# Row maxima of two heads in 64-row pairs, with the odd heads' keys turned round in SBUF

## The reference

```
q, k = rotary(x @ wq.T), rotary(x @ wk.T)          # 4 x 16 heads x 1024 x 64
scores = q @ k.T / 8                               # causal: key <= query
probs  = softmax(where(causal, scores, -inf))      # subtracts each row's maximum
out    = probs @ v
```

## Time and profile before

| | us |
|---|---|
| median of 3 runs | 1261.14 (1259.26 to 1264.67) |
| the profiled execution, its own time | 1261.32 |
| its span | 1259.3 |
| PE busy | 1144.7 (91%) |
| DVE busy | 983.3 (78%) |
| ACT busy | 956.5 (76%) |
| POOL busy | 947.3 (75%) |

### The profile page before, as it was taken

The page is one execution under the profiler, slowest core; times in us unless marked ns, Lnnn a source line. Parts: engine busy times, 40 slices in busy tenths (PEclk is TensorE's granted clock), DMA queues, the critical chain, the costliest instruction groups (busy, mean ns, idle before and its releaser), DMA issues. The chain is left out here.

```text
span 1259.3 us, 34888 instructions
## 1 busy us (share of the span) xinstructions
PE 1144.7 (91%) x13543; PEld 788.8 (63%) x13543; DVE 983.3 (78%) x2220; ACT 956.5 (76%) x2193; POOL 947.3 (75%) x984
## 2 busy tenths in 40 slices
PE   4689999999999999999999999999999598999996
PEld 1256676676767676767667676767777454566553
DVE  7798777787868797878778787979674559867987
ACT  3667888878787878787887879787979665766574
POOL 3578889889888989898988889898767475334463
PEclk8699999999999999999999999999999899999998
DMA  6652425243351515152515334251602100000011
GB/s 201 147 135 52 123 65 129 60 118 82 89 127 43 133 38 136 37 134 69 129 49 128 83 87 118 53 135 35 153 2 65 51 2 1 1 1 1 2 35 34
DMA packets 50660, 97.03 MB, mean 77 GB/s; under 512 B 6720, under 2 KB 23360, under 8 KB 48448
## 3 DMA queue, kind: packets, MB, share of 16 engines
q1 hardware_dynamic: 50496, 94.81, 30.2%
HBM read 58.47 MB, written 34.60 MB: 74 GB/s over the span
## 5 line engine op out<-in xcount | busy, mean ns | idle before, releaser
L807 POOL TENSOR_TENSOR Plo<-P,Phi 128x512 f16<-128x512 f32 (+3 forms) x640 | 538.3, 866 | 129.2 <-ACT P L498 128.6
L495 ACT ACTIVATE Phi<-psS 128x512 f16<-128x512 f32 (+3 forms) x768 | 384.0, 500 | 149.5 <-PE psS L353 105.9
L498 ACT ACTIVATE P<-psS 128x512 f32<-128x512 f32 (+3 forms) x640 | 307.0, 480 | 0.0
L347 PE MATMUL psS<-Q,K 128*128 128x512 f16 (+3 forms) x768 | 252.0, 328 | 40.5 <-DVE Plo L654 37.1
L374 PE MATMUL psO<-V,Plo 128*128 128x65 f16 x2304 | 288.7, 194 | 0.0
L370 PE MATMUL psO<-V,Phi 128*128 128x65 f16 x2304 | 287.5, 192 | 0.0
L372 PE MATMUL psO<-V,Phi 128*128 128x64 f16 x2304 | 286.6, 192 | 0.0
L703 DVE TENSOR_REDUCE pmax<-psX 128x1 f32<-128x512 f32 x384 | 252.9, 684 | 23.0 <-PE psX L434 14.3
L370 PEld LDWEIGHTS psO<-V,Phi 128*128 128x128 f16 x2304 | 219.5, 98 | 56.6 <-issue 0.4
L350 PE MATMUL psS<-Q,K 65*128 65x512 f16 (+3 forms) x768 | 252.2, 328 | 0.0
L434 PE MATMUL psX<-K,Q 128*128 128x512 f16 (+4 forms) x768 | 227.5, 332 | 11.7 <-DMA Q<-HL 3.8
(11 more groups left out here) (200 smaller groups left out, 2161.1 us busy)
## 6 DMA issues: line engine op xcount, KB each, us to landing
K<-k_way SPq DMA_DIRECT2D x48, 512.0 KB, 7.0
k_way<-HL SPq DMA_DIRECT2D x64, 256.0 KB, 3.7
q_way<-HL SPq DMA_DIRECT2D x60, 256.0 KB, 3.7
Q<-q_way SPq DMA_DIRECT2D x60, 256.0 KB, 7.1
Q<-q_way SPq DMA_DIRECT2D x15, 512.0 KB, 11.9
out<-y SPq DMA_DIRECT2D x8, 256.0 KB, 2.2
y<-in_x SPq DMA_DIRECT2D x3, 512.0 KB, 10.8
hn<-in_x SPq DMA_DIRECT2D x3, 512.0 KB, 5.5
```

What stands on the lines that cost most here:

```text
L347: nc.tensor.matmul(out, M.K1[:, p, h, j * P:(j + 1) * P], M.Q1[:, p, h, c:c + w], start=True, stop=False)
L495: nc.scalar.activation(M.Phi[:, U % NP_, 0:w], X, ACT.Exp, scale=SCALE)
L498: nc.scalar.activation(full, X, ACT.Exp, scale=SCALE).then_inc(S.exp_done, 1)
L807: nc.gpsimd.tensor_tensor(M.Plo[:, U % NP_, 0:w], M.P32[:, U % NP_, 0:w], M.Phi[:, U % NP_, 0:w], ALU.subtract).then_inc(S.lo_pool, 1)
```

## The change

The odd heads' keys are loaded turned round, low rows on partitions 0 to 63 and high rows on 64 to 127. This takes three transfers of keys for two heads where one stood, and the same bytes. The full 128-row products of the scores are the same sum in another order. The four banks of `MAXB` that hold a single product of 512 columns without a diagonal (`PAIRED`, banks 4 to 7) are made with the high rows alone: for an even head from partitions 0 to 63, for the odd head beside it from 64 to 127, the one directly behind the other (`both_heads`). The low half of the keys is left out of these products. The even head's item waits for both banks, then both products are issued. The first group's maxima (s < 0) are as before. In `plan()` the items of two heads alternate, and both items of a pair stand at the step of the first.

```diff
--- before.py
+++ after.py
@@ -70,6 +70,7 @@
 NMIX = 3
 assert sorted((t, j + i) for bank in MAXB for t, j, n in bank for i in range(n)) == [
     (t, j) for t in range(TT) for j in range(t + 1)]
+PAIRED = [k for k, bank in enumerate(MAXB) if [j + n - 1 < t for t, j, n in bank] == [True]]
 LO_LAG = 0
 LAG = 5
 NP_ = 6
@@ -128,15 +129,17 @@
                     at.setdefault(V_FIRST[tp], []).append((s, "v", tp))
                 else:
                     put(s, V_STEPS[tp], ("v", tp))
-            for h in range(GH):
-                for k in range(len(MAXB)):
-                    if s < 0:
-                        slot, u = MX_FIRST_GROUP[h]
+            if s < 0:
+                for h in range(GH):
+                    slot, u = MX_FIRST_GROUP[h]
+                    for k in range(len(MAXB)):
                         at.setdefault((slot, u + k), []).append((s, "mx", h, k))
-                    else:
-                        first, last = MX_SECOND if s == 0 else (MX_FIRST, MX_LAST)
-                        i = h * len(MAXB) + k
-                        put(s, first + i * (last - first) // (GH * len(MAXB) - 1), ("mx", h, k))
+            else:
+                first, last = MX_SECOND if s == 0 else (MX_FIRST, MX_LAST)
+                for i in range(GH * len(MAXB)):
+                    pair, k, odd = i // 2 // len(MAXB), i // 2 % len(MAXB), i % 2
+                    own = i - odd if k in PAIRED else i
+                    put(s, first + own * (last - first) // (GH * len(MAXB) - 1), ("mx", 2 * pair + odd, k))
             if s < 0:
                 for h in range(GH):
                     at.setdefault(MT_FIRST[h], []).append((s, "mt", h))
@@ -374,6 +377,23 @@
                     mm = nc.tensor.matmul(O, M.Plo[:, U % NP_, k * P:(k + 1) * P], V[:, HD:2 * HD + 1],
                                           start=False, stop=j == t, skip_group_check=True)
                 mm.then_inc(S.weighted_done, 1)
+
+            def both_heads(item):
+
+                s, kind, h, k = item
+                p = (s + 1) % 2
+                other = (s, kind, h + 1, k)
+                if number[other] >= NAUX:
+                    pe.wait_ge(S.aux_free[bank(other)], number[other] // NAUX)
+                c = 0
+                for t, j, n in MAXB[k]:
+                    for x, low in ((item, 0), (other, HD)):
+                        mm = nc.tensor.matmul(M.psX[:, bank(x), c:c + n * P],
+                                              M.Q1[low:low + HD, p, x[2], t * P:(t + 1) * P],
+                                              M.K1[low:low + HD, p, x[2], j * P:(j + n) * P], start=True, stop=True)
+                        if (t, j, n) == MAXB[k][-1]:
+                            mm.then_inc(S.aux_ready, 1)
+                    c += n * P
 
             def side(item):
                 s, kind, *a = item
@@ -426,7 +446,11 @@
                             pe.wait_ge(S.first_k, 32)
                             pe.wait_ge(S.first_q[h // 2], 16 * GH)
                         else:
-                            pe.wait_ge(S.near_in[h // 2], 48 * (s + 1))
+                            pe.wait_ge(S.near_in[h // 2], 80 * (s + 1))
+                    if s >= 0 and k in PAIRED:
+                        if h % 2 == 0:
+                            both_heads(item)
+                        return
                     c = 0
                     rows = HD if s < 0 and h == 0 else P
                     for t, j, n in MAXB[k]:
@@ -902,7 +926,9 @@
                 sp.wait_ge(S.q_out, 16 * GH * (s + 1))
                 for i in range(2):
                     h = slice(2 * i, 2 * i + 2)
-                    sp.dma_start(M.K1[:, p, h], krows[:, h]).then_inc(S.near_in[i], 16)
+                    sp.dma_start(M.K1[:, p, 2 * i], krows[:, 2 * i]).then_inc(S.near_in[i], 16)
+                    sp.dma_start(M.K1[0:HD, p, 2 * i + 1], krows[HD:P, 2 * i + 1]).then_inc(S.near_in[i], 16)
+                    sp.dma_start(M.K1[HD:P, p, 2 * i + 1], krows[0:HD, 2 * i + 1]).then_inc(S.near_in[i], 16)
                     sp.dma_start(M.Q1[0:HD, p, h], qrows[0:HD, h]).then_inc(S.near_in[i], 16)
                     sp.dma_start(M.Q1[HD:P, p, h], qrows[0:HD, h]).then_inc(S.near_in[i], 16)
                 sp.dma_start(M.K2[0:HD, p], krows[0:HD]).then_inc(S.far_in, 16)
@@ -918,7 +944,7 @@
                     sp.wait_ge(S.first_k2, 16)
                 if which == 0 and s >= 0:
                     for i in range(2):
-                        sp.wait_ge(S.near_in[i], 48 * (s + 1))
+                        sp.wait_ge(S.near_in[i], 80 * (s + 1))
                     sp.wait_ge(S.far_in, 32 * (s + 1))
                 for h in range(GH):
                     sp.dma_start(way[:, :, h, :].rearrange("k f n -> f k n"),
```

## The result

The changed kernel takes 1293.71 us (median of 4, 1292.58 to 1295.92), the one before 1260.2 (median of 4): the ratio is 1.0266, with a 95% interval of 1.0248 to 1.0284. That is 33.5 us slower. Forecast were 1278 and a range of 1252 to 1296; the direction was right, and the loss was forecast at half its size.

A forecast was written before the change was run, and what follows sets the result against it. PE alone was taken to bound steps 8 to 39, sharing the rest with ACT and POOL. Waits of 13 x 1.63 us plus 0.6 made 21.8; a quarter back left 16.4, so 1261.3 became 1278, range 1252 to 1296.

The forecast's parts named there:

- I take a quarter back: Over the groups, a quarter of the 21.8 us loss returns in PE's existing waits, leaving 16.4 us.
- A pair costs 0.43 us: At each pair on PE: 0.43 us against 0.44 for two full products, range 0.22 to 0.54.
- a count of clocks: At each switch to or from 64 rows: 0.05 to 0.057 us at 2.4 GHz, against 0.11 if a time.
- Step 18: At the pair, PE waits 0.84 us a group for DVE to free the first projection's bank.
- Step 19: At the wo item, PE waits 0.1 us at most for the second projection's bank; not counted.
- Step 21: At the wo item, PE waits 0.59 us a group for the bank of step 20's values' product.
- Step 32: Bank 5's pair waits for the first reduce of step 31: 0.2 us a group, 0 to 0.54.
- Steps 15 and 16: No PE wait forecast here; only DVE's low halves delayed 0.6 us at step 16, costing nothing or up to 0.3 a group.
- Loads: Two more load issues ahead of a group's first queries: nothing, at most 0.8 us a group where landing is late.
- one behind the other: Rival: a pair's products don't overlap and cost 0.13 to 0.23 us more than today; 1291, up to 1295 us; chance 0.12.
- absorbed and paying: Rival: PE's waits behind step 39 absorb the 1.63 us and each pair saves 0.10; 1249 us; chance 0.17.
- half and half: Rival: half of the new waits are absorbed (0.8) and each pair saves 0.05; 1266 us; chance 0.15.

The follow-up runs named there:

- e8: The changed kernel with the second wo product at step 22 instead of 21: 1285.34 us, ratio 1.0203 to the kernel before.
- e2: The kernel before with only the odd heads' turned keys, loaded in three transfers for one: 1259.95 us, ratio 0.9997.
- e4: The changed order with both products of a pair on rows 0 to 63, keys not turned, loads of before: 1303.57 us, ratio 1.034 to the kernel before.
- e7: The changed kernel with the first of step 18's two projections at step 17: 1294.84 us, ratio 1.0278 to the kernel before.
- e11: The changed kernel with the pairs of bank 5 one step later (16 to 17, 32 to 33): 1299.92 us, ratio 1.0324 to the kernel before.
- e1: The changed order and common wait, but both products of a pair over all 128 rows, keys and loads of before: 1293.87 us, ratio 1.0262 to the kernel before.
- e3: The kernel before with the 16 products a group that the change pairs each made alone over 64 rows: 1295.32 us, ratio 1.0268.
- e5: The changed kernel with its pairs at every second step (15 to 21 and 31 to 37): 1263.28 us, ratio 1.0031 to the kernel before.
- e6: Pairs at every second step as in e5, but full 128-row products, keys and loads of before: 1266.33 us, ratio 1.0061 to the kernel before.

## Why the prediction was right, and what was off

- *PE is the bound in steps 8 to 39, so a wait there costs its length*: right. "I take a quarter back" was about right in size, 0.4 us a group: the waits for score banks fell from 30.4 to 23.9 us, 0.5 a group. But it came back at step 31 (0.34 here), and nothing behind step 34 (2.42 there, 2.45 at step 47), where the prediction saw most of these waits.
- *A pair costs 0.43 us, which is no gain*: right. The two switches are 0.10 each and the second weight adds nothing; the reading "a time" held, and "a count of clocks", behind the rival that was to be 1249 us, didn't. The range of 0.22 to 0.54 held the value. Missed was that a wait can hide the switch into the pair, as at step 15: a pair there costs 0.32.
- *Step 18*: forecast 0.84 us. The step grew by 1.11 (0.36 to 1.47), of which 0.16 is the pair in the place of one masked product (0.43 against 0.27): 0.95.
- *Step 19*: a wait of 0.1 at most for the second projection's bank, "not counted". It is about 0.15 (by the table, 0.16: the difference fell by 0.06 where a product of 0.22 had left the step).
- *Step 21*: forecast 0.59. The loss grew by 0.67 from step 20 to 22, though a product of 0.22 has left step 21 and a pair has taken the place of one at step 20 (0.21 more): 0.68 or so. e8 took away 8.4 us, 0.65 a group.
- *Step 32*: forecast a net 0.20, in a range to 0.54. At equal work (steps 22 and 34) the loss went from 2.08 to 2.42. With the 0.34 that came back at step 31 that is some 0.7 lost at step 32: the reduce of step 30 that DVE still had before it was not counted.
- *Steps 15 and 16*: missed, 0.36 us by step 18. The prediction named 0.6 us more for DVE at step 16, but not the pair's second bank, that of the first reduce of step 15: some 0.3. The rest is the wait at step 15, 0.22 us for the reduce of step 14, less the 0.1 of the switch that it hides.
- *Loads*: right, nothing (e2).
- *The signs*: as forecast. PE waits 0.9 us for the first projection and 0.5 for the values once a group, the two products of a pair start together, the matmul behind them 0.32 later. The distance between two groups' loads grew from 57.9 to 60.5 us (439.52 to 499.98); forecast was 59.2.

The mechanism was right and the terms of the sum too small: 0.36 + 0.95 + 0.16 + 0.68 + 0.7 = 2.85 us in this group instead of 1.63. Less what came back that is 2.85 - 0.34 = 2.5, instead of 1.63 - 0.41 = 1.22. Over the 13 groups the mean is 2.27 against 1.22, 14 us more, and the group s = 14 cost 2.2 instead of 0.45. That makes 15.4 of the 17 us.

That 1294 lies within the range at all is luck. For this mechanism by itself the prediction gave 1270 to 1288, and 1288 with nothing back and the loads late. The upper end of 1296 lies that high only for the rival of the pairs running one behind the other (up to 1295), which e4 refutes.

What I had not seen is that the waits hang on one chain of DVE work, from the reduces of step 15 to the values of step 20: each was priced against the trace of before, with DVE as late as it was there, and e7 and e11 show that taking one link away lengthens another.

The rivals: "absorbed and paying" and "half and half" fall with the table (0.34 of 2.85 us is absorbed, where they needed half or all) and with e1 (the pairs pay nothing in this order), "one behind the other" with e4.

## What to carry to other kernels

Where a few banks are handed round in order between two engines, two items issued together need both banks at the time of the first, so the second has less time for its bank to be drained; before counting what a merged product saves, list for each item which item three (or N) back must have been drained, and how long the other engine takes for that. A single pair of 64-row products among full ones saves just what its two switches cost. Here it gained only 0.1 us, and only where a wait of PE hid the switch into it; whether several pairs in a row gain was not tried. And a wait removed from such a chain should be measured with the others in place, since it may only move.

## What the runs showed of the hardware

- Going from 128-row to 64-row products and back costs 0.10 us each way at 2.4 GHz (e3), about the same as at 1.2 GHz (0.09 to 0.11); on the way back no weight is loaded ahead. Where PE waits for a bank ahead of the 64-row product, the way in can cost nothing (e5 against e6). The Trainium skill says that a change of tiling mode drains the engine (TensorEngine Tiling (Array Packing), Key Properties); e3 agrees with it, with 0.2 us more for each of 240 lone products.
- Two products of 64 rows and 512 columns on different halves end within 0.39 us of their common start, like one; on the same half, 0.59 (e4). This agrees with what the Trainium skill says of tiles in different rows, that they run together (TensorE: Matmul & The Clock Gate, Part 3).
- A weight of 32 columns between full ones showed no such cost: the next matmul starts 0.11 us after its product.
